# A relational graph layer on one core: nine of eleven matrix products in seven half-size block products, the update vector in DRAM, edge sums in three sweeps

## What is computed

```python
def _rgcn(x, edge_index, edge_type, weight, root, bias):
    src, dst = (edge_index[0], edge_index[1])
    msgs = x[src]
    out = x @ root + bias
    for r in range(weight.shape[0]):
        mask = (edge_type == r).astype(x.dtype)
        sums = jax.ops.segment_sum(msgs * mask[:, None], dst, num_segments=n)
        cnt = jax.ops.segment_sum(mask, dst, num_segments=n)
        mean = sums / jnp.maximum(cnt, 1.0)[:, None]
        out = out + mean @ weight[r]
    return out
...
h = jnp.maximum(_layernorm(x, axis=-1), 0.0)
u = _rgcn(h, edge_index, edge_type, weight, root, bias)
z = jnp.concatenate([u, h], axis=1) @ w_gate + b_gate
return x + jnp.tanh(u) * z + h * (1.0 - z)
```

## Time and profile before

| | us |
|---|---|
| median of 3 runs (lowest, highest) | 1475.69 (1470.72, 1476.54) |
| span of the profiled execution | 1474.3 |
| PE busy (share of the span) | 1376.4 (93%) |
| POOL busy | 645.6 (44%) |
| DVE busy | 628.1 (43%) |
| ACT busy | 330.3 (22%) |
| DMA, mean over the span | 141 GB/s |

### The profile page before, as it was taken

One profiled execution on the slowest core, in us unless ns is written; L12 is line 12 of the kernel. 1 busy time (PEld: TensorE's weight loads), 2 busy tenths in 40 slices (PEclk: granted clock), 3 DMA queues, 4 the chain that ended last, 5 costly groups with the idle time before them and its releaser, 6 DMA issues.

```text
span 1474.3 us, 19978 instructions
## 1 busy us (share of the span) xinstructions
PE 1376.4 (93%) x6658; PEld 737.9 (50%) x6658; DVE 628.1 (43%) x902; ACT 330.3 (22%) x409; POOL 645.6 (44%) x1006
## 2 busy tenths in 40 slices
PE   3966999999999599899999999999999999899898
PEld 1433454566544245454445454544544556566565
DVE  6666767512213223332344234223422343556686
ACT  5434212211132103110311121121203110323200
POOL 2411004867778554644554446544544455530000
PEclk9988999999999799999999999999999999999999
DMA  8422231230321454347545634744464457521875
GB/s 320 129 86 72 92 132 44 63 109 1 115 59 47 150 192 137 110 131 248 153 142 165 212 124 145 251 154 128 153 231 153 131 163 252 163 82 50 207 196 149
DMA packets 68918, 207.95 MB, mean 141 GB/s; under 512 B 17890, under 2 KB 18393, under 8 KB 68836
## 3 DMA queue, kind: packets, MB, share of 16 engines
q1 hardware_dynamic: 35428, 124.42, 24.8%
q0 software_dynamic: 33408, 82.40, 20.0%
HBM read 170.84 MB, written 56.58 MB: 154 GB/s over the span
## 4 chain that ended last, share of the span: by engine, by line
PE 62%; POOL 15%; issue 9%; DMA 7%; DVE 4%; ACT 2%; POOLq 1%; SPq 0%; DVEq 0%; ACTq 0%
PE ps L955 50%; POOL table_rows L359 13%; PE ps L889 9%; DMA reg<-y_rows,idx 6%; POOL onehot L398 1%; DVE u L612 1%; PE ps L945 1%; PE ps L921 1%; DMA W<-in_x_dram 0%; DVE u L616 0%; ACT reg L456 0%; POOL reg L391 0%; DVE ework L659 0%; PE ps L878 0%; PE ps L879 0%
## 5 line engine op out<-in xcount | busy, mean ns | idle before, releaser
L955 PE MATMUL ps<-W,hT 128*128 128x512 f16 (+2 forms) x5232 | 1165.7, 382 | 29.9 <-ACT hT L466 24.1
L955 PEld LDWEIGHTS ps<-W,hT 128*128 128x128 f16 (+2 forms) x5232 | 571.8, 111 | 575.7 <-ACT hT L466 25.5
L391 POOL DMA_INDIRECT reg<-y_rows,idx x196 | 213.1, 1087 | 218.5 <-PE ps L892 164.1
L690 DVE SCALAR_TENSOR_TENSOR yhl<-ps,yhl 128x1024 f16<-128x1024 f32 x80 | 97.9, 1224 | 422.6 <-ACT yhl L520 422.5
L359 POOL DMA_INDIRECT table_rows<-ints x160 | 194.3, 1214 | 147.9 <-issue 147.9
L520 ACT ACTIVATE yhl<-ps 128x1024 f16<-128x1024 f32 x80 | 81.9, 1024 | 780.5 <-PE ps L955 780.4
L889 PE MATMUL ps<-reg,onehot 128*125 x784 | 196.6, 390 | 39.4 <-POOL onehot L398 33.5
L398 POOL TENSOR_SCALAR onehot<-iota_d,dcol 128x125 f16<-128x125 f16 x180 | 121.5, 675 | 161.3 <-DMA reg<-y_rows,idx 157.7
L889 PEld LDWEIGHTS ps<-reg,onehot 128*125 x784 | 100.9, 139 | 98.2 <-issue 50.4
L604 DVE SCALAR_TENSOR_TENSOR W<-W,wsc 128x1024 f16<-128x1024 f32 x88 | 110.4, 1295 | 1.4 <-ACT W L445 1.2
L445 ACT ACTIVATE W<-W,wsc 128x1024 f16<-128x1024 f32 x88 | 96.2, 1140 | 59.2 <-PE ps L955 54.3
(11 more groups left out here) (131 smaller groups left out, 487.3 us busy)
## 6 DMA issues: line engine op xcount, KB each, us to landing
y_rows<-yhl SPq DMA_DIRECT2D x72, 512.0 KB, 3.4
W<-in_L_gnn_weight_dram SPq DMA_DIRECT2D x64, 512.0 KB, 9.5
W<-in_L_gnn_w_gate_dram SPq DMA_DIRECT2D x16, 512.0 KB, 8.7
reg<-in_x_dram SPq DMA_DIRECT2D x9, 512.0 KB, 4.2
hs_rows<-reg SPq DMA_DIRECT2D x9, 512.0 KB, 5.1
zh_rows<-reg SPq DMA_DIRECT2D x10, 448.0 KB
W<-zh_rows SPq DMA_DIRECT2D x10, 448.0 KB
W<-hs_rows SPq DMA_DIRECT2D x10, 448.0 KB
```

The source lines that it names most:

```text
L391: pool.indirect_dma_start(out=G[:, b, :], out_offset=None, in_=y_rows[rel], in_offset=bass.IndirectOffsetOnAxis(ap=idx[:, b, :], axis=0), ...
L690: nc.vector.scalar_tensor_tensor(out=yhl[0:rows, m % 2, D:2 * D], in0=whole, scalar=2.0 ** -Y_BITS, in1=yhl[0:rows, m % 2, 0:D], op0=ALU.mult,
L955: last = nc.tensor.matmul(ps[0:rows, b + half, :], hT[:, v_h, k, n0:n0 + rows], Wh[:, HOME[w][k], v_w, half * HC:(half + 1) * HC], start=( ...
```

## The change

**Units.** PE's work is now counted in units: 20 for rel0 and gate_u (a row tile by one half of the output, 24 matmuls), and 35 for each of the nine others. Unit n takes PSUM bank n mod 4 and waits until the unit four before it was evacuated. rel0 has units 0 to 19, rel1 20 to 54, root 55 to 89, rel2 to rel7 90 to 299, gate_h 300 to 334, gate_u 335 to 354.

**Seven block products.** The nine products between are split in 2 x 2 blocks of 640 (padded) x 512 by 512 x 512, and computed as seven block products in place of eight, of sums and differences of the blocks (`winograd`): 7 phases x 5 row tiles x 4 contraction blocks x 3 = 420 matmuls instead of 480. The four sums of the left side are made once, by GpSimd (`add_sums`, `low_sums`) and ACT; the four of each weight by DVE (`sum_quadrants`), and seven 512 x 512 matrices are split instead of four. Outputs come from running sums in `Q`, `V` (SBUF, float32) and `C`: `finish` on DVE reads PSUM 35 times for a relation product (six of the seven phases, one of them twice; the first phase is copied by ACT), the four output blocks are then split by ACT (L777) and DVE (L1023).

**Edge ranks.** The scans are cut in five chunks of 16 groups (`scan_chunk` in units 26, 32, 38, 44, 50); the ranks within rows are scanned on DVE, offset on ACT (80 small activations) and gathered to one position per edge on GpSimd (`ranks`); one small matmul replaces the 27 pairs. The positions are finished at unit 64, the 160 indirect DMAs follow, and DVE waits for the table at unit 156.

**Three sweeps.** `u` is in DRAM (`u_rows`), with three tiles in SBUF (`ub`). Groups are ordered by target tile within a sweep: relations 0 to 3 (40 groups after units 164 to 247), 4 and 5 (20 groups after units 250 to 299), 6 and 7 (20 groups after units 305 to 329). Each sweep loads and stores each tile of `u` once. The gathers of a sweep wait until the y rows of its last relation are stored. Padding to whole turns of the ring is done per sweep: 192 table tiles, where there were 196. y rows are stored as half rows, 1 KB pieces. gate_u's preparation reads tanh(u) from DRAM as a fourth operand.

```diff
+    SWEEPS = [(0, 4), (4, 6), (6, 8)]
+    NS = len(SWEEPS)
...
-    AGG_FROM, AGG_LAST = 2 * 39 + 1, 2 * slot(W_GH, 1) + 1
-    AGG_AT = [AGG_FROM + g * (AGG_LAST - AGG_FROM) // (NG - NJ) if g < NG - NJ else AGG_LAST + g - (NG - NJ) for g in range(NG)]
...
+    PH = 7
+    FIRST = [0] + [2 * NJ + PH * HT * (w - 1) for w in range(1, NW)]
+    NU = FIRST[W_GU] + 2 * NJ
...
+    A11, A12, S2, S3, S1, S4, A21, A22 = range(8)
+    LHS = [A11, A12, S2, S3, S1, S4, A22]
...
+    AGG_AT = ([164 + g * 86 // 40 for g in range(40)] + [250 + g * 52 // 20 for g in range(20)]
+              + [305 + g * 26 // 20 for g in range(20)])
...
+    U_DONE = {STEP_END[FINAL + j]: j for j in range(NJ)}
+    TURN_U = {STEP_END[FINAL + j] + 4: j for j in range(NJ)}
...
-    y_rows = [nc.dram_tensor(f"y_rows{r}", [N, 2 * D], F16).ap() for r in range(R)]
+    y_rows = [nc.dram_tensor(f"y_rows{i}", [(r1 - r0) * N, 2 * D], F16).ap() for i, (r0, r1) in enumerate(SWEEPS)]
...
+            CONV_AT[w] = [FIRST[w] + d for d in (-5, -3, 2, 6, 11, 16, 21)]
+            SUM_AT[w] = [FIRST[w] + d for d in (0, 1, 4, 8)]
...
+    TOTALS_AT, BOUNDS_AT = 20, 24
+    SCAN_AT = {26: 0, 32: 1, 38: 2, 44: 3, 50: 4}
+    PLACES_AT, TABLE_AT = 64, AGG_AT[0] - 8
```

The sweeps' loads and stores on SP, and GpSimd's sums and ranks:

```diff
+            def load_u(k):
+                sweep, j = STEPS[k]
...
+                    of = k - NJ
+                    sp.wait_ge(s[f"u_stored{of % 3}"], 32 * (of // 3 + 1))
+                for n0, p0, rows in halves(*DTL[j]):
+                    sp.dma_start(ub[p0:p0 + rows, k % 3, :], u_rows[n0:n0 + rows, :]).then_inc(s[f"u_loaded{k % 3}"], 16)
+
+            def store_u(k):
+                sweep, j = STEPS[k]
+                if sweep < NS - 1:
+                    sp.wait_ge(s["u_added"], SPAN[sweep][0] + (j + 1) * (SWEEPS[sweep][1] - SWEEPS[sweep][0]))
+                else:
+                    sp.wait_ge(s["tanh_ready"], j + 1)
+                for n0, p0, rows in halves(*DTL[j]):
+                    sp.dma_start(u_rows[n0:n0 + rows, :], ub[p0:p0 + rows, k % 3, :]).then_inc(s[f"u_stored{k % 3}"], 16)
 
...
+                    for k in range(2):
+                        load_u(k)
+                for k in range(len(STEPS)):
+                    if n == STEP_END[k] + (2 if k < FINAL else 4):
+                        store_u(k)
+                        if k + 2 < len(STEPS):
+                            load_u(k + 2)
+                if n < FIRST[W_GU] and out_no(n) is not None:
...
+                pool.tensor_tensor(a1, h(A22, 0), a4, ALU.add).then_inc(s["pool_step"], 1)
+                steps[0] += 1
+                step(pool.tensor_tensor(a3, h(A11, 0), a4, ALU.subtract))
...
+            def low_sums(i):
+                pool.wait_ge(s["s_high"], i + 1)
+                pool.tensor_tensor(hT[:, S2:S4 + 1, 1, :, cols(i)], sbuf_s, hT[:, S2:S4 + 1, 0, :, cols(i)],
+                                   ALU.subtract).then_inc(s["s_low"], 1)
...
+            def ranks(c):
+
+                pool.wait_ge(s["pos3_ready"], c + 1)
+                step(pool.tensor_tensor(rank3, rank3, hot3[:, c % 2, :, :], ALU.mult))
+                n = CG // 2
+                while n:
+                    last = pool.tensor_tensor(rank3[:, 0:n, :], rank3[:, 0:n, :], rank3[:, n:2 * n, :], ALU.add)
+                    n //= 2
...
+                for b in range(4):
+                    pool.wait_ge(s[f"y_stored{b}"], 16 * 2 * NJ * (W_OF[SWEEPS[i][1] - 1] + 1) // 4)
```

DVE: quadrant sums, scans, and the evacuation of a unit:

```diff
+                    dve.wait_ge(s["w_lo"], conv_no(w, c - 1) + 1)
+                to, first, second, op = ((b12, b22, b12, ALU.subtract), (b11, b12, b11, ALU.add),
+                                         (b21, b11, b21, ALU.subtract), (b11, b22, b11, ALU.subtract))[c]
...
+            def scan_chunk(c):
+                b = c % 2
...
+                    dve.wait_ge(s["ranked"], c - 1)
+                    dve.wait_ge(s["cum_ready"], c - 1)
+                step(chunk_hot(hot3[:, b, :, :], c))
+                if c:
+                    dve.wait_ge(s["pos3_ready"], c)
+                    dve.wait_ge(s["cum_ready"], c)
+                step(nc.vector.tensor_tensor_scan(out=cum, data0=hot[:, b, :], data1=hot[:, b, :], initial=0.0,
...
+                def scaled(to, scale, of):
+                    return nc.vector.scalar_tensor_tensor(out=to, in0=part, scalar=scale, in1=of, op0=ALU.mult, op1=ALU.add)
...
-                    nc.vector.scalar_tensor_tensor(out=zbuf[0:rows, j % 2, :], in0=whole, scalar=wscale(w, 1)[0:rows],
-                                                   in1=brow[0:rows, :], op0=ALU.mult, op1=ALU.add).then_inc(s["evac"], 1)
+                if p == 1 and w in REL:
+                    dve.wait_ge(s[COPIED], FREED[n - HT][1])
+                elif p in (1, 3, 4, 5):
+                    dve.wait_ge(s[EVAC], FREED[n - HT][1])
+                dve.wait_ge(s["gemm_done"], n + 1)
+                if p == 2:
+                    scaled(Q[:, i, :], c, Q[:, i, :]).then_inc(s[EVAC], 1)
+                elif p == 3:
+                    scaled(V[:, i, :], c, Q[:, i, :]).then_inc(s[EVAC], 1)
+                else:
+                    of, scale = (Q if p in (1, 5) else V)[:, i, :], cn if p == 6 else c
+                    to = o_to[:, o % 4, :]
+                    dve.wait_ge(s[YDONE], o - 3)
+                    if n == unit(1, 1, 0):
+                        dve.wait_ge(s["w_lo"], conv_no(1, 3) + 1)
+                    if w not in REL:
+                        close(to, scale, of)
...
+                        scaled(to, scale, of)
+                        scaled(Q[:, i, :], c, Q[:, i, :]).then_inc(s[EVAC], 1)
+                    else:
```

PE: a unit of 12 matmuls, and the loop:

```diff
+            def product(n, m, n0, rows, w, c, k, first, stop):
+
+                for v_h, v_w in ((0, 0), (0, 1), (1, 0)):
+                    last = nc.tensor.matmul(ps[0:rows, n % 4, :], hT[:, m, v_h, k, n0:n0 + rows], Wh[:, MAT[w][c], v_w, k, :],
+                                            start=(first and v_h + v_w == 0), stop=(stop and v_h == 1))
...
+            def winograd(n):
+                w = w_of(n)
+                p, i = divmod(n - FIRST[w], HT)
+                if i == 0:
+                    pe.wait_ge(s["w_lo"], conv_no(w, p) + 1)
+                if w == 1 and p == 2:
+                    pe.wait_ge(s["s_low"], i + 1)
+                for k in range(KH):
...
-                    if t == BOUNDS:
-                        group_sums()
-                    for g in AGG.get(2 * t + 1, ()):
-                        sum_group(g)
+            for n in range(NU):
+                if n >= 4:
+                    pe.wait_ge(s[FREED[n - 4][0]], FREED[n - 4][1])
+                if w_of(n) in (0, W_GU):
+                    half_tile(n)
...
+                if n == TOTALS_AT:
+                    totals()
+                if n == BOUNDS_AT:
+                    group_sums()
+                for g in AGG.get(n, ()):
+                    sum_group(g)
```

1194 lines of the change are left out of this document (705 added, 489 removed).

## The result

The changed kernel takes 1616.5 us (median of 4 runs, 1611.6 to 1622.7) where the kernel before takes 1474.2 us: 1.096 times as long, 95% interval 1.093 to 1.099. The forecast was 1420 with a range of 1340 to 1500, so the sign was wrong too. The profiled execution has a span of 1617.9 us, 199 more than the 1419 of the working.

A forecast was written before the change was run, and what follows sets the result against it. The prediction took TensorE as the bound nearly everywhere; PE alone would save 132 us, ending near 1342. A timeline of PE's waits for DVE, table and gathers ended at 1419, plus 1.4: 1420 us, range 1340 to 1500.

The forecast's parts named there:

- What PE saves: Whole kernel: fewer product matmuls (117 us), rank matmuls (11) and table tiles (3.6) save PE 132 us.
- Step 1: rel0, units 0 to 19: no change, bounds -10 and +10 us; unit 20 starts at 174 us.
- Step 2: rel1, units 20 to 54: DVE is the bound, 118 us including 10 for GpSimd's disturbance.
- Rival C: Products: DVE's program order makes units wait, 5 us lost in each of nine, 1465 us; chance 0.12.
- The way to the scatter: Nine units of root after rel1: 23 us, so the scatter starts at 315 us.
- Step 3: Table: scatter 254 us plus 26 for DVE's disturbance, first edge sum at 617 us, PE's stall about 40.
- Steps 4 and 5: Sweeps one and two: gathers at 3.34 us per tile bind the first, to 934; hidden in the second, to 1128.
- Rival B: Sweeps: added traffic slows the gather loop, 3.9 us per tile and 1500 us as middle; chance 0.20.
- Step 6: Third sweep, units 305 to 329: gathers bind at 160 us, plus 2 for their start and 5 for late u.
- The sign that the prediction gave: If right, PE waits for GpSimd's L645 mostly in the last 48 tiles, 2 to 4 us a tile.
- Step 7: gate_u: 104 us of matmuls, 2 of waits, 4.3 of tail, 110 us; DMA share 0.85 still under full.
- Rival A: rel1, scatter and sweeps: gathers keep up at 2.9 us per tile, DVE's work hides, about 1326 us; chance 0.23.

The follow-up runs named there:

- e9: Changed kernel with the edits of e2, e3, e5 and e8 together; outputs not the reference's: 1422.0 us, 0.965 of the kernel before.
- e16: As e1, with DVE's scans and ScalarE's offsets kept, GpSimd's product and additions of each rank chunk replaced by a small fill: 1552.6 us.
- e1: Changed kernel with the 160 scatters left out and the table filled with made-up rows at the start; rank chunks stay: 1588.1 us.
- e15: As e1, with DVE's five scan chunks kept, ScalarE's offsets and GpSimd's rank chunks left out: 1539.0 us.
- e2: As e1, with scan chunks, GpSimd's rank chunks and ScalarE's offsets left out too: 1511.2 us.
- e5: Changed kernel with every gather bringing 2 KB of a row instead of 4 KB; outputs not the reference's: 1565.9 us.
- e3: Changed kernel with the third sweep's tile of u fetched two units after a step's end instead of four: 1603.7 us.
- e6: Changed kernel with the third sweep's tiles of u not fetched from DRAM; outputs not the reference's: 1603.4 us.
- e8: Changed kernel with gate_u's weight splits 2 to 4 one unit earlier and three of four tile operands fetched before the store's landing: 1595.7 us.

## Why the prediction was wrong, step by step

**What PE saves.** Right in the count (4740 matmuls) and, where the clock is up, in the price: 444 of them took 97.64 us in gate_u, 0.220 each for 0.216. Of the 132 us forecast, 73 are seen in PE's busy time (106 in e9, where it waits less). They did not reach the end, since PE is the bound in few stretches now.

**Step 1, rel0.** Right: unit 20 starts at 168 us for 174, inside the bounds.

**Step 2, rel1: the step that failed first.** Forecast 118 us, measured 173. The failure is in "DVE is the bound here", from which the step took the length of the stretch: neither DVE nor PE was busy all the time. DVE was busy 128 us and idle 45, and an idle time had no term. The sum of DVE's work was 108 + 10; the 10 us for GpSimd's disturbance, "between 0 and 25", measured 24 (e16 against e1), at the upper end of its bounds. The rest is order. A scan of 8.3 us and more stands ahead of evacuations for which PE had 10.4 us of banks: 26 us (e15 against e2). ScalarE's offsets, 5.2 us a chunk, stand ahead of its other work: 13 us (e16 against e15). And 20 us of PE's waits are there in e2 with no rank work at all, 9.4 of them behind GpSimd's block sums, which the prediction had named in step 1 and priced at nothing in this one. It asked of each engine how much, and not who stands behind a wait in whose program. Rival C is this kind of mechanism, but it was priced at 5 us a product, placed in the weight's scale, and never applied to the ranks or the block sums.

**The way to the scatter** took 43 us for 23: the last chunk ended only at 361 us and the places stand at unit 64.

**Step 3, the table.** The length of the term was right: 284 us for 280, and 30 for 22 up to the first sum; PE's stall there, forecast at about 40 us, was 39.09. The start was 69 us late, from step 2. The 26 us for disturbance by DVE were weighed against the Trainium skill (SBUF — State Buffer, Who interferes with whom), by whose inference the scatter would have lost nothing and stayed at 254. 254 to 284 speaks against the inference, and so do the single rows: a scatter of 1.19 us took 3.10 beside a DVE sum of weight blocks, both of whose inputs are in SBUF. The scatter also reads its places from SBUF, so which part of it waited stays open. But that the 26 us came so near was luck. The step read the late start of one scatter as DVE's doing and put all 14 us that the scatter lost before on DVE. At 1.49 us a scatter that trace loses 17: 13 are the gaps before every 40th scatter, three of the four without such DVE work beside them, and 4 are lengthened scatters, 4 / 27 = 0.15 us per us of DVE work. In the changed kernel it was 36 / 91 = 0.40. The 0.33 of 79 us that the step took happened to fall near that.

**Steps 4 and 5, sweeps one and two.** 577 us for 511: by PE's matmuls 356 for 317 in the first sweep, 221 for 194 in the second. In the first the mechanism, gathers as the bound, was right, and said to be so "by a little". The term mis-sized is the pace, 3.34 us per tile. It came from one run of 17 gathers before, at a DMA share of 0.60, and was carried to stretches where the share is 0.67 and the landing 5.0 us for 4.6. Measured: 3.78 in the first 96. The prediction wrote that the new traffic "is not priced in the sum"; e5 prices half of the gathers' own bytes at 50 us over the three sweeps, and 0.26 us of the 0.44 by which a tile was mis-sized. In the second sweep "the gather 160: hidden" fell: PE was busy 204 us of the 221 and waited 17 for tiles. Rival B is shown in its mechanism. Its size, 3.9 us and 1500, was not far off, but it was a rival to steps 2 and 7 and not a term beside them.

**Step 6, the third sweep.** 191 us for 167. "5 us for its late ones" was the load of u: 29.8 us of PE's waits, worth 13 us of time (e3, e6). The rest is pace (4.10 us per tile for 3.34) and clock: 0.85 granted in this window. The sign that the prediction gave, waits for L645 mostly in the last 48 tiles, did not come: they are 40.0 us in the first sweep and 18.4 in the third.

**Step 7, gate_u.** 130 us for 110, and 22 for 14 ahead of it. The failed sentence is that a DMA share of 0.85 is "still under full". The share was 0.78 and DVE waited all the same, as a share says nothing of a ring whose turn is a chain of store, landing and four loads. e8 took out the 20 us by order alone: there the share is 0.87 and gate_u takes 109 us, so the queues could carry the forecast's load.

**The clock** had no term. A wait of PE can cost twice, once itself and once by slower matmuls behind it: the granted clock fell from 0.979 to 0.919, and against e9 PE's busy time is 33 us longer.

**Rival A** (gathers keep up, DVE hides) fell with steps 2 and 4. **The sign** hung on all errors lying on the same side. The forecast's stages are in series, and the rivals held a price for most of them, but the chances were given to one at a time. Failures of B, of C's kind and of step 7 came together. B's 80 us over the forecast and C's 45 together would have been 1545, still 70 short.

## What to carry to other kernels

When work moves to an engine that sits idle half the time, follow the wait it brings and list what stands behind that wait in each engine's program; the sum of busy times is then only a lower bound. To tell a wait from a slowdown, leave the neighbour's work out and compare both the busy and the idle time of the engine for the same instructions. A change that removes matmuls from a bound engine is worth them only up to the next chain: draw that chain (here first gather, pace, last gather, tail) and price the change on it before counting matmuls. And where several stages in series can each come out late, add their likely losses instead of choosing one.

## What the runs showed of the hardware

- Gathers of 4 KB rows land in 5.0 us (median) in sweeps that move about 200 GB/s, their own bytes included, in 3.6 us when only 2 KB of a row are fetched; writing y in pieces of 1 KB or of 2 KB makes no difference (5.0 and 5.1 us).
- GpSimd's indirect scatters of one element per partition took 1.19 us each where DVE ran nothing with two SBUF inputs, and up to 3.3 us beside such a DVE instruction. 160 of them were busy 194 us before and 226 us in the changed kernel.
- The same 109 DVE instructions of rel1 took 107 us with GpSimd's rank sums left out and 131 beside them (e16, e1).
- The GpSimd additions of one rank chunk, the same instructions each time, took 6.7 to 15.5 us in rel1. Beside GpSimd's product of the last chunk a DVE subtraction of 512 columns took 5.18 us where most take 0.68. The row of DVE, then that of GpSimd:

```profile
346.81 5.18 DVE L1023 TENSOR_TENSOR yhl<-W,yhl 128x512 f16<-128x512 f32 x1 [1.65 <-ACT yhl L777]
```

```profile
346.40 5.04 POOL L579 TENSOR_TENSOR early<-early 125x2560 f32<-125x2560 f32 x1 [18.92 <-ACT early L752]
```

The product ended at 351.4 us and the subtraction at 352.0: one engine can hold the other up for a whole instruction. By the Trainium skill (SBUF — State Buffer, Who interferes with whom), a DVE instruction with two SBUF inputs contends with a GpSimd instruction that reads SBUF; the rows agree.
